# Maxima over 128 neighbouring queries, and eight 512-byte transfers of them a group instead of two of 2048

## The reference

```python
# a: q, k, v = einsum(norm(x), kernel[0..2]); 16 heads of 64
scores = jnp.einsum('bhsd,bhtd->bhst', q, k) * scale
attn = jax.nn.softmax(scores, axis=-1)
out = jnp.einsum('bhst,bhtd->bhsd', attn, v)
# b: the same with q = rope(up_q(down_q(h))), k = rope(up_k(down_kv(h)))
```

## Time and profile before

| | |
|---|---|
| runs (3), us | 3993.34, 3990.06, 3994.79; median 3993.34 |
| the profiled execution, us | 3990.85, its span 3989.1 |
| TensorE clock granted, mean | 0.974 |
| attention a, from the first maxima to the last projection | about 104 to 1791 us |
| attention b | about 2142 to 3774 us |
| DMAs issued for maxima | 256, of 2 KB, 2.0 us to landing |

### The profile page before, as it was taken

The page is one execution under the profiler, slowest core; times in us unless marked ns, Lnnn a source line. Parts: engine busy times, 40 slices in busy tenths (PEclk is TensorE's granted clock), DMA queues, the critical chain, the costliest instruction groups (busy, mean ns, idle before and its releaser), DMA issues. The chain is left out here.

```text
span 3989.1 us, 59212 instructions
## 1 busy us (share of the span) xinstructions
PE 3718.3 (93%) x16736; PEld 2499.7 (63%) x16736; DVE 2264.7 (57%) x2984; ACT 1698.3 (43%) x3212; POOL 2623.0 (66%) x1471
## 2 busy tenths in 40 slices
PE   2899999999999999987874999999999999999799
PEld 2666666666666666646763566666666666666488
DVE  4444444444444444436654677777777777777344
ACT  1344444444444444434431444444444444444344
POOL 2577777777777777863213677777777777778511
PEclk9999999999999999998986999999999999999899
DMA  5444444344444444311014455555555455554100
GB/s 172 109 105 106 106 98 99 98 98 105 106 106 105 101 100 104 84 26 35 32 53 107 99 102 100 102 102 103 104 102 103 99 103 102 102 103 82 40 17 27
DMA packets 312425, 363.64 MB, mean 91 GB/s; under 512 B 144545, under 2 KB 182305, under 8 KB 308257
## 3 DMA queue, kind: packets, MB, share of 16 engines
q1 hardware_dynamic: 303808, 291.43, 35.0%
q10 hardware_dynamic: 8544, 71.31, 5.1%
HBM read 138.68 MB, written 21.50 MB: 40 GB/s over the span
## 5 line engine op out<-in xcount | busy, mean ns | idle before, releaser
L860 POOL TENSOR_TENSOR a_rs<-a_rs,a_p 128x1024 f32<-128x1024 f32 x384 | 914.6, 2382 | 287.8 <-ACT a_p L773 270.4
L787 DVE TENSOR_REDUCE a_nmax<-a_ps_x 128x1 fp32r<-128x1024 f32 x512 | 627.1, 1225 | 771.4 <-PE a_ps_x L605 771.4
L860 POOL TENSOR_TENSOR b_rs<-b_rs,b_p 128x1024 f32<-128x1024 f32 x384 | 915.8, 2385 | 219.1 <-ACT b_p L773 200.5
L787 DVE TENSOR_REDUCE b_nmax<-b_ps_x 128x1 fp32r<-128x1024 f32 x512 | 626.8, 1224 | 370.1 <-PE b_ps_x L605 332.5
L773 ACT ACTIVATE a_p<-a_ps_s 128x512 f32<-128x512 f32 x1024 | 528.9, 603 | 400.0 <-PE a_ps_s L619 375.3
L773 ACT ACTIVATE b_p<-b_ps_s 128x512 f32<-128x512 f32 x1024 | 529.2, 603 | 359.6 <-PE b_ps_s L619 337.7
L635 PE MATMUL a_ps_o<-a_p,a_v 128*64 128x512 f32 x2048 | 467.7, 598 | 0.0
L635 PE MATMUL b_ps_o<-b_p,b_v 128*64 128x512 f32 x2048 | 467.7, 598 | 0.0
L605 PE MATMUL b_ps_x<-b_k,b_q 128*128 128x512 f32 x1024 | 395.3, 468 | 35.2 <-DMA b_q<-b_nat_l 18.9
L618 PE MATMUL b_ps_s<-b_q,b_k 128*128 128x512 f32 x1024 | 415.6, 406 | 2.8 <-ACT b_p L773 1.6
L618 PE MATMUL a_ps_s<-a_q,a_k 128*128 128x512 f32 x1024 | 414.3, 405 | 1.1 <-DMA a_q<-a_nmax 1.1
(11 more groups left out here) (166 smaller groups left out, 5722.1 us busy)
## 6 DMA issues: line engine op xcount, KB each, us to landing
a_k<-a_nat_h SPq DMA_DIRECT2D x256, 128.0 KB, 2.4
a_q<-a_nat_h SPq DMA_DIRECT2D x256, 128.0 KB, 2.4
b_k<-b_nat_h SPq DMA_DIRECT2D x256, 128.0 KB, 3.8
b_q<-b_nat_h SPq DMA_DIRECT2D x256, 128.0 KB, 3.6
feat<-feat_a ACTq DMA_DIRECT2D x15, 2048.0 KB, 8.9
feat<-feat_b ACTq DMA_DIRECT2D x15, 2048.0 KB, 11.2
a_k<-a_nat_l SPq DMA_DIRECT2D x128, 128.0 KB, 2.4
a_q<-a_nat_l SPq DMA_DIRECT2D x128, 128.0 KB, 2.4
```

The source lines that it names most:

```text
L787: dve.reduce_max(nmax[:, g % 2, head, qi:qi + 1], ps_x[:].rearrange("p a b -> p (a b)"), AX_X, negate=True).then_inc(s_red, 1)
L860: pool.tensor_tensor(out, out, p[:, bb, i, :], ALU.add).then_inc(s_sum, 1)
```

## The change

Three things, in both attentions. The stationary operand of a maxima step is 128 neighbouring queries, `qi * P` to `(qi + 1) * P`, instead of every fourth. `nmax`'s column `qi` then holds the maxima of that stretch, and `shift` issues two DMAs for each `qi`, one a head: 128 partitions of one number into 128 neighbouring numbers of `q2`. And SP waits for reduction 6 of the group's 8, issues the six DMAs of `qi` 0 to 2, waits for the eighth and issues the last two. The waits on `s_shift` count eight DMAs a group.

```diff
-                mm = pe.matmul(ps_x[:, half, :], q1[:, slot, head, qi:BLOCK:BT],
+                mm = pe.matmul(ps_x[:, half, :], q1[:, slot, head, qi * P:(qi + 1) * P],
                                k1[:, pair % 2, head, half * BLOCK:(half + 1) * BLOCK], start=True, stop=True)
...
-                pe.wait_ge(s_shift, due(t, 128, 32 * (u + 1)))
+                pe.wait_ge(s_shift, due(t, 512, 128 * (u + 1)))
...
-                dve.wait_ge(s_shift, due(t, 128, 32 * (g - 1)))
+                dve.wait_ge(s_shift, due(t, 512, 128 * (g - 1)))
...
-        def shift(sp, g, head):
-
-            sp.dma_start(q2[0:1, g % 4, head, :].rearrange("o (p a) -> o p a", a=BT).bitcast(F32),
-                         nmax[:, g % 2, head, :].bitcast(F32)).then_inc(s_shift, 16)
+        def shift(sp, g, qi):
+
+            for head in range(2):
+                sp.dma_start(q2[0:1, g % 4, head, qi * P:(qi + 1) * P].unsqueeze(2).bitcast(F32),
+                             nmax[:, g % 2, head, qi:qi + 1].bitcast(F32)).then_inc(s_shift, 16)
...
             if live(t, 4, u + 1, NGROUP):
+                sp.wait_ge(s_red, due(t, 32, 8 * (u + 2) - 2))
+                for qi in range(BT - 1):
+                    shift(sp, u + 1, qi)
                 sp.wait_ge(s_red, due(t, 32, 8 * (u + 2)))
-                shift(sp, u + 1, 0)
-                shift(sp, u + 1, 1)
+                shift(sp, u + 1, BT - 1)
```

## The result

The changed kernel is slower: 4024.7 us, median of four runs (4019.2 to 4030.8), against 3994.1 for the kernel before (3990.1 to 3995.0) on the same chip, a ratio of 1.0077 (95% interval 1.0061 to 1.0093). The forecast was 3929.0, and its range ended at 3956.

A forecast was written before the change was run, and what follows sets the result against it. TensorE, busy 93% of the span, was taken to bound the kernel. Profiled 3990.9 us, minus 63 from exposed loads, nothing for transfers, plus 1 (half the profiled-to-median difference) gave 3929; range 3912 to 3956.

The forecast's parts named there:

- The load's length: Maxima weight load L605: 314 ns with every fourth column would become about 188 ns with neighbouring columns, a difference of 126 ns.
- The price of an exposed load: First maxima matmul behind float32 matmuls on TensorE: 0.47 us becomes 0.34 (values, row sums), 0.44 becomes about 0.32 (projection).
- The term of a: TensorE in attention a: 142 x 0.13 = 18.5 us plus 120 x 0.12 = 14.4 us, together 33 us gained.
- b's share: TensorE in attention b: 299 exposed loads x 0.13 = 39 us, less 6 and 3 lost, leaving 30 us gained.
- three exposed loads lie between that load's issue and the end of this wait: Feature load to wait for q's copies, once a body in b: 15 x 3 x 0.13 = 6 us of gain lost.
- part 1: Neighbouring queries in the maxima's weight loads on TensorE: 63 us gained in all, bounds 37 to 75.
- SP's issues cost nothing: Six more issues a group, 3.5 us, hide in SP's wait for the last reduction; uncovered, 450 us over 128 groups.
- The landing in the steady state: Last two maxima transfers land 2.0 us after issue's start, at most 3.1; slack 1.1 us in a, 0.6 in b.
- The rival that ended on the slow side: 4-byte pieces land late, first scores wait on `s_shift`; at 4 us landing it costs 137 us, giving 4065; chance 0.06.
- The sentence that failed: Early six transfers have landed before the last two, except behind the feature load once a body, where TensorE is late; unpriced.
- part 2: Maxima transfers on SP: eight a group instead of two, six early, in 4-byte pieces; issue costs nothing, landing stays 2.0 us.
- 0.01 us at 460 places: Upper bound's extra: maxima loads in a stream also hold TensorE back slightly, some 3 us more gain.

The follow-up runs named there:

- e1: Kernel before with only the maxima's stationary operand as 128 neighbouring queries, old transfers kept (exponent scaled, output not the reference's): 3959.0 us, ratio 0.9909.
- n1: Kernel before without the 15 loads of the next features inside each attention's loop: 3964.1 us, ratio 0.9918.
- n2: Changed kernel without the 15 loads of the next features inside each attention's loop: 3910.6 us, ratio 0.9787.
- d1: Kernel before plus six dummy transfers a group, each 2 KB from one row to another in a few long pieces: 4007.0 us, ratio 1.0030.
- e2: Changed kernel with the old every-fourth-query columns, so only the eight 4-byte-piece transfers are new (exponent scaled, output not the reference's): 4054.6 us, ratio 1.0146.
- d4: Kernel before plus six early dummy transfers a group, each of 128 pieces of 4 bytes: 4053.9 us, ratio 1.0147.
- d16: Kernel before plus six early dummy transfers a group, each of 128 pieces of 16 bytes: 4053.3 us, ratio 1.0145.
- m2: Changed kernel with new columns and 4-byte transfers for odd heads only; in b's feature-load window all five transfers follow the last reduction: 3971.6 us, ratio 0.9946.

## Why the prediction was wrong, step by step

**The load's length: right.** A median of 188 ns in both attentions, from 309, for the reason given. The rule of the Trainium skill cited there ("Advanced Engine Details and Errata", SBUF Cachelines) agrees with this row, and the one on columns alone ("TensorE: Matmul & The Clock Gate", LDWEIGHTS) does not; that page says nothing of spacing, which is the prediction's reading of it.

**The price of an exposed load: right where the load waited, wrong behind the projection in a.** 0.465 became 0.337, as forecast. For the 120 loads of a behind L661, which no wait row lists, the forecast had 0.44 becoming 0.32, from L289 behind the transposes in the earlier trace rows; it measured 0.420. The sentence that holds is the prediction's own, that a load that waits is exposed: these didn't wait. Nor is it the shape of the matmuls ahead, since behind the same ones in b, where the loads wait, 0.465 became 0.336. Why a load that starts at once leaves 0.42, these runs don't show. Of the 120 x 0.12 = 14.4 us, 120 x 0.02, about 2, are left. The term of a, 33 us, measured 16.6 (e1).

**b's share: the price right, the deduction too small.** Forecast were 39 - 6 - 3 = 30 us. Without the feature load b gains 29 (n1 and n2); that this is so near 30 is partly luck, since 6 us of the deduction are for the feature load, and without them 36 were due. With the load b gains 8.3 (e1). The step that failed is "three exposed loads lie between that load's issue and the end of this wait", priced at 6 us: TensorE runs its whole body ahead into this wait, and 11.5 us come back as a longer wait for the copies of `q`. The clock can hold the other 9 or so: 24 us more at half clock cost an estimated 12 at most (half of what it works there). How much of them is the clock, no run tells apart. So part 1 is worth 35 us by the medians of e1, 25 by the maxima spans of the two profiled executions, and not 63.

**SP's issues cost nothing: nearly right.** Six more issues a group cost 13.5 us where their pieces are few (d1), not the 450 of an uncovered issue. But 13.5 isn't nothing: it is in b (0.9 us a body), again in the window of the feature load, where the last maxima land 2 us later.

**The landing in the steady state: right.** 2.0 us. The 23 waits of the scores for it (14 in a, 9 in b) lie 14 to 19 us after a feature load's issue and, one each, at the ends of the blocks. The rival that ended on the slow side had the right sign and the wrong place: it priced the 109 steady groups at 137 us, and they cost none.

**The sentence that failed**: the early six "have [landed], except behind the feature load, once a body, where TensorE itself is late". The exception was seen and written off with a half sentence and no number. It costs 1.1 us a body in a and 2.6 in b against e1, 56 us over 15 bodies each, and e2 has 61. Two things were wrong in it. That TensorE is late there took the old lateness as a cover; but of what TensorE is late for there, `rinv` and the normalization behind it became later with the pieces: that wait rose from 15.0 to 31.6 us, and is 16.0 in e1, with the new columns alone, and 35.0 in e2, with the transfers alone. (The wait for the copies of `q` rose as well, from 18.9 to 31.4, but nearly all of that is part 1's gain given back: 30.4 in e1, 22.8 in e2.) And the landing of the two last was bounded by 3.1 us, the longest in a trace with 256 pieces of maxima a group; with 1024, in this window of b, the last lands 8.4 us behind the last reduction. Together, against e1, b's waits for the normalization, the copies and the maxima are 27.5 us longer and its half clock 37.6, an estimate of up to 19 us of work; its bodies are 40 us longer. Bodies, not groups, were the place to look for it: a body that is 2.6 us longer, 15 times, weighs as much as 0.36 us in each of the 109 steady groups.

**The sum, again with what was measured**: 3991 - 35 (part 1) + 61 (part 2) = 4017 from the profiled execution, where the change measured 4019.2. (Two slips in the prediction's bounds bear on nothing: 0.01 us at 460 places is 4.6 and not 3, and the lower end of the range takes a gain of 78 where the text has 75.)

What stays open is how the pieces take their time in the queue. Each packet of 4 bytes shows 9 ns in the trace, yet in the window above six transfers of 128 pieces, eight on each of the core's 16 DMA engines if they are spread evenly, landed 0.3 to 0.5 us apart, which is an estimate of 40 to 60 ns a piece, also after the 2 MB load had landed. "DMA: Bandwidth & Descriptors" of the Trainium skill, section "Why small descriptors are slow (HBM only)", says that SBUF to SBUF transfers do not suffer from small descriptors; d4, d16 and d1 here disagree as soon as such transfers queue beside a large load, and agree with it where nothing else is queued (2.0 us to landing with 4-byte and with 16-byte pieces).

## What to carry to other kernels

When a change multiplies the pieces of a DMA, price them in the window where that queue is fullest, by name: what stands behind and beside them, who waits for each, and how late the last lands; a median landing of 2 us says nothing of it. Before a strided weight load is mended everywhere, find which loads are exposed: in a they all belonged to the odd head, and half of the change with the transfers moved behind the large load in b (m2) made the kernel 0.5% faster where the whole made it 0.8% slower. And a gain on an engine that once in each loop body waits for a transfer issued in that body is kept only if that transfer moves with it.

## What the hardware showed that was not expected

- A 128x128 weight load of float32 numbers takes 309 ns (median) where its columns lie 16 bytes apart and 188 where they are neighbours, in one and the same kernel too (m2 has both).
- What a slow load costs TensorE depends on whether the load had to wait, not on the matmuls it stands behind. Behind L661 (256 columns) in a, where 116 of 120 loads start within 60 ns of the load before, the next matmul takes 0.437 us with the long load and 0.419 with the short; behind the same matmuls in b, where 108 of 120 loads waited longer, 0.465 and 0.336; behind L635 (512 columns) 0.465 and 0.337. In a stream it takes 0.23 with either.
- 768 more pieces a group cost 61 us in the kernel beside a 2 MB load in each body, 4-byte and 16-byte pieces alike (1.0147 and 1.0145), and nothing measurable in windows without that load (24.4 us in b and 27.1 in a in the changed kernel and in e1 alike). Six transfers with the same bytes in few pieces cost 13.5 us.
- Splitting the large load's pieces from 16 KB to 2 KB let the copies of `q` beside it land 2 us earlier (9.4 for 11.4 after its issue in b), and the load itself 2 us later (13.2 for 11.2): the wait moves to the large load, 22.0 us in b without the small pieces and 78.9 with them.
- TensorE's clock, at 2.4 GHz in the steady windows, was granted at 1.2 for 3.4 to 10.2 us at a time in b's window of the feature load, twice in the kernel before (6.8 us in all, with 35 us of waits for transfers, the normalization and the maxima in b) and 12 times in the changed one (68.3 us, with 75 us of them); so a wait that grows can cost more than its length.
